# Shared gating steps moved into the routing chain of a macaron MoE kernel, with the rank product and the Exp moved to fit

## The chip, the cores and the metric

One core of a Trainium2 chip runs the whole program. The metric is the device time of one execution in microseconds (us); lower is better. The engines are TensorE (PE in the profile, PEld for its weight loads), VectorE (DVE), ScalarE (ACT), GpSimd (POOL) and the DMA queues, which SyncE (SP) and GpSimd fill. Each engine runs its own instructions in their written order and waits on semaphores that others raise.

## The reference

The input is 16 sequences of 256 tokens with 128 features, 4096 tokens in all. Three residual blocks follow each other:

```
x = x + 0.5 * ffn(layernorm(x))
x = x + attn(layernorm(x))
x = x + 0.5 * ffn(layernorm(x))

def ffn(h):                               # the same weights both times
    probs = softmax(h @ gate_W.T)         # 8 experts
    top_v, top_i = top_k(probs, 2)
    routed = sum over the 2 chosen experts e of
             top_v * (silu(h @ w1_e) * (h @ w3_e)) @ w2_e      # 128 -> 512 -> 128
    shared = (silu(h @ w1_s) * (h @ w3_s)) @ w2_s / 8          # 8 shared experts, 512 wide together
    return 0.5 * shared + 0.5 * routed
```

The attention is a linear one with running sums; the change does not touch it.

## The kernel before

The 4096 tokens lie in 32 tiles of 128, and 4 tiles are a chunk, so there are 8 chunks. The two feed-forward layers (l = 0 and 1 in the code, the first and the second layer here) have the same stages:

1. **Normalise and score.** Each chunk is normalised (DVE), transposed (PE), copied (ACT), multiplied with the gate (PE), and its scores are copied to `logit` (ACT). ACT and POOL split the transposed tokens into a high and a low part (`high_xnT`, `low_xnT`).
2. **The front.** Two kinds of work are interleaved. One is the shared expert in steps: a step k is one chunk times one quarter of the 512 hidden features. PE makes six matmuls for it (`in_shared`: three into psG, three into psU), ACT takes Silu of psG (`silu_shared`), DVE multiplies Silu by psU (`gated_shared`, reached by `shared_steps`), and after four steps PE makes the out-product of the chunk (`out_shared`, 32 matmuls), which DVE adds to X (`add_shared`). PE starts step k only when the Silu and the product of step k-2 are done, since psG and psU have two buffers. The other is routing: DVE finds the largest and second largest score of each token (`first_of` and its neighbours), PE counts ranks (`rank`), DVE turns ranks into slots (`slots_of`), 16 batches of one-hot matrices (DVE `batch`, ACT `pairs`, PE `batch`) put each token's number into its slot, and `table` and `experts` make the lists from them. In the first layer DVE also makes eight low parts of the routed weights behind the table (`low_part`), one per step, out of eight high parts that ACT made (W13H, L1213).
3. **The routed stage.** POOL fetches token rows by the table, PE transposes and multiplies them with the weights that ACT copies out of W13H and W13L (`weights_of`, L1229), and POOL sends the results back.
4. The last steps of the shared expert (4 in the first layer, 8 in the second) cover the tail.

The front has 28 steps in the first layer, of which 4 are done during the normalisation (`TAKEN` = 4 and 0), and 24 in the second. The order is written out by hand with constants. `PLAN` gives after which step DVE makes which batches (16 in 11 steps); ACT makes its part one step later, and PE takes the batches up `PLAN_LAG` = 3 steps later. `TABLE_STEP` is the step after which DVE makes the table. `RANK_STEP` is the step of PE at which `rank` stands; `out_shared` of the chunk c stands on PE at step 4c + 5. `Chain.then` lets DVE wait for each routing operation before the next.

Within the DVE chain of routing the kernel before has 2 shared steps between the maxima, 1 behind the gates (the softmax sum, its reciprocal and two products, L819 to L822) and 1 in `slots_of`. On ACT the two Exp of the scores stand behind the first Silu of the front (L1200 to L1203), in front of the second. On PE:

```
if 5 <= k < front[l] + 5:
    out_shared(Step.of(k - 5, 2 * FT))
if k == RANK_STEP[l]:        # 5 and 3
    rank()
```

Of the kernel before, what the change touches and what calls it, by code (L numbers as in the profile page):

```python
# [14 lines left out]
D = 128  # L15
# [39 lines left out]
RANK_STEP = [5, 3]  # L55

PLAN = [{n + 4 + step: 2 - step % 2 if step < 10 else 1 for step in range(11)} for n in TAKEN]
PLAN_LAG = 3
TABLE_STEP = [n + 15 for n in TAKEN]
# [36 lines left out]
ALU = mybir.AluOpType  # L96
# [66 lines left out]
def macaron(nc, x, w_qkvT, w_swigluT, w_outT, gateT, w1_e, w3_e, w2_e, w1_s, w3_s, w2_s, out):  # L163
    ctx = ExitStack()
    with ctx:
# [542 lines left out]
        def _(dve):  # L708
# [34 lines left out]
            for l in range(2):  # L743
# [47 lines left out]
                def first_of(k, scores):  # L791
# [11 lines left out]
                dve.wait_ge(shifted, l + 1)  # L803
                first_of(0, cand[:, :, :])
# [7 lines left out]
                first_of(1, logit[:, :, :])  # L812
                route.then(dve.tensor_tensor(chosen[:, :, :].rearrange("p e i -> p i e"), onehot[0][:, :, :],
# [4 lines left out]
                dve.wait_ge(expd, l + 1)  # L818
                route.then(dve.tensor_reduce(row_a[:, :], prob[:, :, :], X_AXIS, ALU.add))  # L819
                route.then(dve.reciprocal(row_b[:, :], row_a[:, :]))  # L820
                dve.tensor_scalar(XN[:, :, D], row_b[:, :], 0.25, None, ALU.mult)
                dve.scalar_tensor_tensor(XN[:, :, D + 1], row_b[:, :], 0.25, second_exp[:, :], ALU.mult, ALU.mult)\  # L822
                   .then_inc(gates_done, 1)
                shared_steps(1)

                def slots_of():
# [19 lines left out]
                    for k in range(TOPK):  # L846
                        route.then(dve.tensor_tensor(pick[:, :, :], cum[:, :, :].rearrange("p e i -> p i e"),
                                                     onehot[k][:, :, :], ALU.mult))
                        route.then(dve.tensor_reduce(posf[:, k, :], pick[:, :, :], X_AXIS, ALU.add))
                    route.then(dve.tensor_copy(pos[:, :, :], posf[:, :, :]))  # L850
# [83 lines left out]
                for k in range(SHARED):  # L934
                    if k == front[l] + 6 % FT:
                        copy_xT(Step.of(0, 2 * GT))
                    if k == done[0]:
                        shared_steps(1)
                    for _ in range(PLAN[l].get(k, 0)):
                        batch(taken)  # L940
                        taken += 1
                    if k == TABLE_STEP[l]:
                        table()
                        experts()
                    if l == 0 and 0 < k - TABLE_STEP[0] <= 2 * WPARTS:
                        low_part(k - TABLE_STEP[0] - 1)

# [180 lines left out]
        def _(act):  # L1128
            act.wait_ge(consts, CONSTS)
            for l in range(2):  # L1130
# [56 lines left out]
                else:  # L1187
                    high = 0
                    for c in range(TURNED, CHUNKS + 1):
# [6 lines left out]
                        high += 1  # L1196
                    silu_shared(taken)
                    for c in range(high, CHUNKS):
                        high_xnT(Step.of(c, 2))
                act.wait_ge(second_found, l + 1)  # L1200
                act.wait_ge(shifted, l + 1)
                act.activation(prob[:, :, :], cand[:, :, :], ACT.Exp)
                act.activation(second_exp[:, :], second[:, :], ACT.Exp).then_inc(expd, 1)  # L1203
# [3 lines left out]
                for k in range(taken + 1, SHARED):  # L1207
# [3 lines left out]
                    if l == 0 and part < 2 * WPARTS:  # L1211
                        cols = bass.ds(part // 2 * WCOLS, WCOLS)
                        act.activation(W13H[:, part % 2, cols], W13[:, part % 2, cols], ACT.Copy).then_inc(high_made, 1)  # L1213
                    for _ in range(PLAN[l].get(k - 1, 0)):
                        pairs(batches)
                        batches += 1
# [111 lines left out]
        def _(pe):  # L1328
# [19 lines left out]
            for l in range(2):  # L1348
# [88 lines left out]
                for k in range(taken, SHARED + 1):  # L1437
# [3 lines left out]
                    if k < front[l]:  # L1441
                        in_shared(Step.of(k, 2 * FT))
                    if k == front[l] + 1:
# [3 lines left out]
                    if k == RANK_STEP[l]:  # L1447
                        rank()
# [215 lines left out]
```

## Time and profile before

| | us |
|---|---|
| median of 3 runs | 735.5 |
| lowest and highest run | 734.17 and 737.56 |
| span of the profiled execution, first to last instruction | 733.5 |

The profile gives for its own execution the span only; the median of the runs lies 2.0 us above it, and the profile does not tell how much of that lies around the span. Over the span PE is busy 660.3 us (90%), DVE 458.8 (63%), ACT 411.3 (56%) and POOL 430.6 (59%). The first layer's front lies at about 36 to 112 us, its routed stage follows to about 301 us, attention to about 431 us, the second layer's front at 440 to 512 us, and its routed stage to about 701 us.

Times are read on the axis of the span. A timeline row gives the start, the length, the engine, the line and, in brackets, how long the engine stood idle before it and what released it. The length reaches to the end of the last result; on DVE and ACT the next instruction can start somewhat before that.

### The profile page before, as it was taken

What the parts mean: (1) busy time and instruction counts of PE and PEld (TensorE: products, weight loads), DVE (VectorE), ACT (ScalarE), POOL (GpSimd) and SP (SyncE); (2) the same over time, 40 slices, a digit from 0 to 9 for tenths busy, and PEclk for the clock granted to TensorE, in tenths of its full rate; (3) what the DMA queues carried; (4) which work ended last, traced back from release to release, by engine and by line L of the source; (5) the groups of instructions that cost most, each with busy time, mean ns of one, the idle gap of its engine ahead of it and who ended that gap; (6) DMA issues with size and microseconds to landing.
All of it is one profiled execution on the core that took longest, in us unless ns stands there. A gap on an engine that the chain in (4) does not pass through costs nothing.

```text
span 733.5 us, 14294 instructions
## 1 busy us (share of the span) xinstructions
PE 660.3 (90%) x4860; PEld 602.1 (82%) x4860; DVE 458.8 (63%) x1177; ACT 411.3 (56%) x861; POOL 430.6 (59%) x511
## 2 busy tenths in 40 slices
PE   3878999999999999957987777999999999999995
PEld 3767879999999999825654574888999999999983
DVE  6678895554445555359999867884555555544536
ACT  2658617666666666236654436664666666666520
POOL 5600075777777776489987424007577777777530
PEclk9989999999999999989999997999999999999999
DMA  9542011221222231131100002402212212212137
GB/s 296 231 78 40 1 42 38 56 52 52 52 55 52 52 53 44 57 105 44 47 12 1 0 1 46 73 2 49 40 55 54 52 52 56 51 53 52 43 104 261
DMA packets 35685, 45.91 MB, mean 63 GB/s; under 512 B 6432, under 2 KB 27936, under 8 KB 35232
## 3 DMA queue, kind: packets, MB, share of 16 engines
q1 hardware_dynamic: 25632, 24.39, 11.8%
q0 software_dynamic: 9984, 20.63, 11.5%
q8 instruction: 40, 0.66, 0.4%
q14 instruction: 29, 0.24, 0.1%
HBM read 28.41 MB, written 16.58 MB: 61 GB/s over the span
## 4 chain that ended last, share of the span: by engine, by line
PE 65%; DVE 20%; issue 4%; ACT 4%; POOL 3%; DMA 2%; SPq 1%; ACTq 0%; POOLq 0%; DVEq 0%
PE psY L1487 18%; PE psG L1334 6%; PE psU L1336 6%; PE psG L1336 6%; PE psU L1335 6%; PE psG L1335 6%; PE psU L1334 6%; PE psH L1405 4%; DVE rec L1076 3%; PE psT L1433 2%; DVE hs L748 2%; DVE XN L738 2%; DVE ln_stats L725 1%; DVE xn L1060 1%; POOL results L641 1%
## 5 line engine op out<-in xcount | busy, mean ns | idle before, releaser
L626 POOL DMA_INDIRECT rows<-tokens,source x156 | 153.7, 985 | 156.3 <-DVE source L900 98.6
L1155 ACT ACTIVATE silu<-psG 128x512 f32<-128x512 f32 x220 | 131.1, 596 | 150.6 <-PE psG L1336 147.2
L954 DVE TENSOR_TENSOR hT<-silu,psU 128x512 f32<-128x512 f32 x156 | 107.4, 688 | 158.9 <-PE psU L1336 150.3
L641 POOL DMA_INDIRECT results<-yout,target x156 | 153.8, 986 | 63.3 <-issue 45.7
L1487 PE MATMUL psY<-W,hT 128*128 x1232 | 162.4, 275 | 1.8 <-DVE yout L980 1.8
L1487 PEld LDWEIGHTS psY<-W,hT 128*128 128x128 f32 x1232 | 150.4, 191 | 2.2 <-DVE hT L954 2.2
L1229 ACT ACTIVATE w_high<-W13H 128x1024 fp32r x78 | 82.7, 1061 | 59.0 <-PE psU L1336 54.8
L1334 PE MATMUL psG<-xTH,w_high 128*128 128x256 f32 x312 | 100.0, 321 | 0.7 <-ACT w_low L1229 0.7
L1336 PE MATMUL psG<-xTH,w_low 128*128 128x256 f32 x312 | 88.0, 282 | 0.0
L1336 PE MATMUL psU<-xTH,w_low 128*128 128x256 f32 x312 | 88.0, 282 | 0.0
L1335 PE MATMUL psU<-xTL,w_high 128*128 128x256 f32 x312 | 87.7, 281 | 0.0
L1335 PE MATMUL psG<-xTL,w_high 128*128 128x256 f32 x312 | 87.4, 280 | 0.0
L1334 PE MATMUL psU<-xTH,w_high 128*128 128x256 f32 x312 | 86.9, 278 | 0.0
L1229 ACT ACTIVATE w_low<-W13L 128x1024 fp32r x78 | 81.8, 1048 | 0.0
L748 DVE TENSOR_TENSOR hs<-silu,psU 128x512 f32<-128x512 f32 x64 | 43.7, 684 | 38.3 <-PE psU L1336 30.5
L1405 PEld LDWEIGHTS psH<-W2S,hs 128*128 128x128 f32 x512 | 59.4, 192 | 5.7 <-DVE hs L748 4.7
L1405 PE MATMUL psH<-W2S,hs 128*128 128x128 f32 x512 | 60.1, 276 | 2.9 <-DVE hs L748 2.9
L1334 PEld LDWEIGHTS psG<-xTH,w_high 128*128 128x128 f32 x312 | 59.2, 190 | 0.9 <-issue 0.9
L1335 PEld LDWEIGHTS psG<-xTL,w_high 128*128 128x128 f32 x312 | 59.3, 190 | 0.0
L1334 PEld LDWEIGHTS psU<-xTH,w_high 128*128 128x128 f32 x312 | 59.1, 190 | 0.0
L1336 PEld LDWEIGHTS psG<-xTH,w_low 128*128 128x128 f32 x312 | 58.8, 188 | 0.0
L1335 PEld LDWEIGHTS psU<-xTL,w_high 128*128 128x128 f32 x312 | 58.6, 188 | 0.0
(188 smaller groups left out, 1215.7 us busy)
## 6 DMA issues: line engine op xcount, KB each, us to landing
W<-w_e SPq DMA_DIRECT2D x3, 2048.0 KB, 13.7
tokens<-XN SPq DMA_DIRECT2D x16, 260.0 KB, 5.9
Y<-results SPq DMA_DIRECT2D x32, 128.0 KB, 2.2
YF<-results SPq DMA_DIRECT2D x16, 256.0 KB, 5.9
rows<-tokens,source POOLq DMA_INDIRECT x156
results<-yout,target POOLq DMA_INDIRECT x156, 2.3
X<-x SPq DMA_DIRECT2D x8, 256.0 KB, 5.5
out<-X SPq DMA_DIRECT2D x8, 256.0 KB, 2.8
```

The source lines that it names most:

```text
L626: pool.indirect_dma_start(rows[:, slot(l, g), t, :], None, tokens, bass.IndirectOffsetOnAxis(ap=source[:, tile:tile + 1], axis=0))\
L641: pool.indirect_dma_start(results, bass.IndirectOffsetOnAxis(ap=target[:, tile:tile + 1], axis=0), yout[:, g % 2, t, :], None).then_inc(y_ ...
L748: dve.tensor_tensor(hidden, silu[:, s.u % 2, :], psU[:, s.u % 2, :], ALU.mult).then_inc(h_done, 1)
L954: dve.tensor_tensor(hT[:, s.u // PT % 2, half, :].rearrange("p f c -> p (f c)"), silu[:, s.u % 2, :], psU[:, s.u % 2, :], ALU.mult).then_i ...
L1076: dve.reciprocal(rec[:, s.u, :, :], den[:, s.u, :, :]).then_inc(y_link, 1)
L1155: act.activation(silu[:, s.u % 2, :], psG[:, s.u % 2, :], ACT.Silu).then_inc(silu_done, 1)
L1229: act.activation(used[p % 2][:, :, :], kept[:, :, bass.ds(entries[p], F)], ACT.Copy)\
L1334: pe.matmul(out, a_high, b_high, start=True, stop=False)
L1335: pe.matmul(out, a_high, b_low, start=False, stop=False)
L1336: return pe.matmul(out, a_low, b_high, start=False, stop=True)
L1405: i = pe.matmul(psH[:, par, t * D:(t + 1) * D], hs[:, par, f, t * P:(t + 1) * P], W2S[:, f, :], start=(f == 0), stop=(f == FT - 1))
L1487: i = pe.matmul(into[:, t * D:(t + 1) * D], hT[:, s.u // PT % 2, f, s.u % PT * P:(s.u % PT + 1) * P], W2[:, bass.ds(at + f * D, D)], start ...
```

## The change

`WOVEN` = 7 shared steps stand in the routing chain of DVE instead of 4: one more ahead of the first `first_of`, one more behind the second, and one more between the two choices in `slots_of`; the step that stood behind the gates now stands behind `picked`. The batches, the table and all that follows come 3 steps later (`PLAN`, `TABLE_STEP`). `rank` moves on PE to the steps 9 and 5 and stands ahead of that step's out-product. In the first layer the Exp move on ACT behind the Silu of step 10, and the gates on DVE behind the batch of step 12. In the second layer one more `high_xnT` and then the one Exp of `cand` stand ahead of the first Silu; the second choice's exponential is no longer an Exp but is picked out of `prob` by two DVE operations, in front of the gates.

```diff
-RANK_STEP = [5, 3]
-
-PLAN = [{n + 4 + step: 2 - step % 2 if step < 10 else 1 for step in range(11)} for n in TAKEN]
+WOVEN = 7
+RANK_STEP = [n + 5 for n in TAKEN]
+
+EXP_STEP = TAKEN[0] + WOVEN - 1
+GATES_STEP = EXP_STEP + 2
+
+PLAN = [{n + WOVEN + step: 2 - step % 2 if step < 10 else 1 for step in range(11)} for n in TAKEN]
 PLAN_LAG = 3
-TABLE_STEP = [n + 15 for n in TAKEN]
+TABLE_STEP = [n + WOVEN + 11 for n in TAKEN]
...
                 dve.wait_ge(shifted, l + 1)
+                shared_steps(1)
                 first_of(0, cand[:, :, :])
...
                 first_of(1, logit[:, :, :])
+                shared_steps(1)
...
-                dve.wait_ge(expd, l + 1)
-                route.then(dve.tensor_reduce(row_a[:, :], prob[:, :, :], X_AXIS, ALU.add))
...
+                def gates():
+
+                    dve.wait_ge(expd, l + 1)
+                    if l == 1:
+                        route.then(dve.tensor_tensor(pick[:, :, :], onehot[1][:, :, :], prob[:, :, :], ALU.mult))
+                        route.then(dve.tensor_reduce(second_exp[:, :], pick[:, :, :], X_AXIS, ALU.add))
+                    route.then(dve.tensor_reduce(row_a[:, :], prob[:, :, :], X_AXIS, ALU.add))
...
                 shared_steps(1)
+                if l == 1:
+                    gates()
...
+                        if k == 0:
+                            shared_steps(1)
...
+                    if l == 0 and k == GATES_STEP:
+                        gates()
...
+                    high_xnT(Step.of(high, 2))
+                    high += 1
+
+                    act.wait_ge(shifted, l + 1)
+                    act.activation(prob[:, :, :], cand[:, :, :], ACT.Exp).then_inc(expd, 1)
                     silu_shared(taken)
...
-                act.wait_ge(second_found, l + 1)
-                act.wait_ge(shifted, l + 1)
-                act.activation(prob[:, :, :], cand[:, :, :], ACT.Exp)
-                act.activation(second_exp[:, :], second[:, :], ACT.Exp).then_inc(expd, 1)
...
+                    if l == 0 and k == EXP_STEP:
+                        exponents()
...
+                    if k == RANK_STEP[l]:
+                        rank()
                     if k == front[l] + 1:
                         transpose_rows(Step.of(0, 2 * GT))
                     if 5 <= k < front[l] + 5:
                         out_shared(Step.of(k - 5, 2 * FT))
-                    if k == RANK_STEP[l]:
-                        rank()
```

## Rows read from the trace of the kernel before

**Rows 1.** Page part 4: shares of the chain of work that ended last, by engine.
```profile
PE 65%; DVE 20%; issue 4%; ACT 4%; POOL 3%; DMA 2%; SPq 1%; ACTq 0%; POOLq 0%; DVEq 0%
```

**Rows 2.** Stretches: start:end length, busy PE PEld DVE ACT POOL, clock, DMA share, GB/s.
```profile
41.70:46.40 4.70, 0.01 (x1) 0.00 (x0) 3.10 (x8) 2.28 (x3) 0.00 (x0) 0.89 0.00 0
46.40:52.00 5.60, 5.58 (x15) 4.43 (x16) 3.23 (x13) 2.83 (x4) 0.00 (x0) 0.50 0.72 153
449.40:458.20 8.80, 8.32 (x20) 5.38 (x21) 8.19 (x24) 2.22 (x4) 0.84 (x1) 0.50 0.44 92
```

**Rows 3.** Timeline, first layer (start, length, engine, line, what, count, [idle before <-releaser]).
```profile
40.60 0.42 ACT L1202 ACTIVATE prob<-cand 128x256 f32<-128x256 f32 x1 [1.55 <-DVE second L808]
43.13 0.69 DVE L748 TENSOR_TENSOR hs<-silu,psU 128x512 f32<-128x512 f32 x1 [2.11 <-ACT silu L1155]
46.41 0.19 PE L1412 MATMUL psY<-chosen_rows,before 128*128 128x8 bf16 x1 [4.71 <-DVE chosen_rows L816]
62.54 0.43 PE L1421 MATMUL psT<-pair,at_place 128*128 128x156 bf16 x4 [0.64 <-ACT pair L1168]
```

**Rows 4.** Timeline, second layer, VectorE, ScalarE and TensorE at the start of the front.
```profile
441.51 1.41 DVE L793 SCALAR_TENSOR_TENSOR pick<-cand,rev_e 128x256 f32<-128x256 f32 x1
447.45 1.28 ACT L1155 ACT_TABLE_LOAD   x1
449.39 0.79 PE L1334 MATMUL psG<-XNTH,W13SH 128*128 128x512 f32 x1 [3.83 <-ACT silu L1155]
460.65 0.48 DVE L866 TENSOR_TENSOR in_tile<-column,pos_part 128x312 bf16<-128x312 bf16 x1
463.47 0.72 PE L1421 MATMUL psT<-pair,at_place 128*128 128x156 bf16 x8
```

**Rows 5.** Timeline, first layer, from the last batch to the first routed matmul.
```profile
88.18 0.45 PE L1421 MATMUL psT<-pair,at_place 128*128 128x156 bf16 x4
88.67 0.24 DVE L889 COPY is_choice<-psT 128x78 f32<-128x78 f32 x1 [1.01 <-PE psT L1421]
92.19 0.69 DVE L748 TENSOR_TENSOR hs<-silu,psU 128x512 f32<-128x512 f32 x1
92.80 1.22 DVE L908 TENSOR_TENSOR W13L<-W,W13H 128x1024 fp32r<-128x1024 f32 x1
107.75 1.22 DVE L908 TENSOR_TENSOR W13L<-W,W13H 128x1024 fp32r<-128x1024 f32 x1
110.17 1.06 ACT L1229 ACTIVATE w_high<-W13H 128x1024 fp32r x1 [4.14 <-issue]
112.42 0.36 PE L1334 MATMUL psG<-xTH,w_high 128*128 128x256 f32 x1 [0.70 <-ACT w_low L1229]
```

**Rows 6.** Timeline, TensorE: an out-product, two steps, and the same end in layer 2.
```profile
89.90 3.73 PE L1405 MATMUL psH<-W2S,hs 128*128 128x128 f32 x32
93.39 0.48 PE L1334 MATMUL psG<-XNTH,W13SH 128*128 128x512 f32 x1
94.86 0.39 PE L1334 MATMUL psG<-XNTH,W13SH 128*128 128x512 f32 x1
490.57 0.45 PE L1421 MATMUL psT<-pair,at_place 128*128 128x156 bf16 x4
512.30 0.36 PE L1334 MATMUL psG<-xTH,w_high 128*128 128x256 f32 x1
```

**Rows 7.** Groups by line: busy us, mean ns | idle before, releasers.
```profile
L1155 ACT ACTIVATE silu<-psG 128x512 f32<-128x512 f32 x220 | 131.1, 596 | 150.6 <-PE psG L1336 147.2 <-DVE hs L748 3.2
L1213 ACT ACTIVATE W13H<-W 128x1024 fp32r<-128x1024 f32 x8 | 8.4, 1050 | 0.0
L1273 ACT ACT_TABLE_LOAD x1 | 1.3, 1283 | 0.0
```

**Rows 8.** Attention: timeline row of a wait, and the stretch right behind it.
```profile
385.82 0.44 PE L1539 MATMUL psT<-ident,xn 128*128 128x128 f32 x2 [2.36 <-DVE xn L1060]
385.82:387.00 1.18, 0.70 (x3) 0.47 (x4) 1.15 (x8) 0.38 (x1) 1.18 (x2) 0.86 0.07 14
```

More of the change, by code:

```diff
@@ L816, in _ @@
                 dve.tensor_copy(chosen_rows[:, :], base[:, :]).then_inc(picked, 1)
-                dve.wait_ge(expd, l + 1)
-                route.then(dve.tensor_reduce(row_a[:, :], prob[:, :, :], X_AXIS, ALU.add))
[L820 to L823, printed above, removed]
+                def gates():
[4 more added lines that the diff above has]
+                    route.then(dve.tensor_reduce(row_a[:, :], prob[:, :, :], X_AXIS, ALU.add))
+                    route.then(dve.reciprocal(row_b[:, :], row_a[:, :]))
+                    dve.tensor_scalar(XN[:, :, D], row_b[:, :], 0.25, None, ALU.mult)
+                    dve.scalar_tensor_tensor(XN[:, :, D + 1], row_b[:, :], 0.25, second_exp[:, :], ALU.mult, ALU.mult)\
+                       .then_inc(gates_done, 1)
                 shared_steps(1)
+                if l == 1:
+                    gates()
                 def slots_of():
@@ L1199, in _, with exponents @@
                         high_xnT(Step.of(c, 2))
-                act.wait_ge(second_found, l + 1)
-                act.wait_ge(shifted, l + 1)
-                act.activation(prob[:, :, :], cand[:, :, :], ACT.Exp)
-                act.activation(second_exp[:, :], second[:, :], ACT.Exp).then_inc(expd, 1)
+                def exponents():
+                    act.wait_ge(shifted, l + 1)
+                    act.wait_ge(second_found, l + 1)
+                    act.activation(prob[:, :, :], cand[:, :, :], ACT.Exp)
+                    act.activation(second_exp[:, :], second[:, :], ACT.Exp).then_inc(expd, 1)
                 if l == 0:
```

## The prediction

> **What bounds the kernel now.** I read the page first: the chain that ended last is 65% TensorE and 20% VectorE [rows 1]. Then I read the busy time by stretch, to find where TensorE stands. In the first layer it stands for the whole of 41.70 to 46.40, and behind that it runs 5.60 us at a granted clock of 0.50, its lower level (1.2 of 2.4 GHz) [rows 2]. That costs about half of 5.60, so 2.8 us. The timeline says why: `rank` waited 4.71 us for the DVE chain, and that chain had itself stood 2.11 us for a Silu that was queued behind the Exp of the scores and the table load [rows 3]. In the second layer TensorE stands 3.83 us for the second Silu, which again is queued behind two Exp and their loads [rows 4], and 8.80 us follow at clock 0.50 [rows 2]. So the change aims at real waits. But a wait of TensorE counts only if what ends the front is TensorE. In the first layer it is not quite: the first routed matmul at 112.42 waits for ACT's weight copy, which waited for the last low part of DVE [rows 5]. In the second layer it is TensorE's own queue, 512.30 [rows 6].
>
> **Prices of the parts.** On TensorE a step is 94.86 - 93.39 = 1.47 us (1.37 behind another step) and an out-product 93.39 - 89.90 = 3.49 [rows 6]. On DVE a shared step takes 92.80 - 92.19 = 0.6 until the next instruction [rows 5]; `add_shared` has the same shape and I give it 0.6 too. On ACT a Silu is 0.60, a W13H part 1.05 [rows 7], a table load 1.28 [rows 4], the Exp 0.42 [rows 3]. Nothing else is computed anew but two DVE operations in the second layer.
>
> **First layer, up to the last batch.** Now DVE makes step 4 ahead of the first maximum and step 5 behind it, so TensorE can go on with steps 6 to 9 during the chain. `rank` moves behind step 9; I get the ranks' input ready about 0.5 us after TensorE arrives, instead of 4.71. That gives 4.2, and the slow stretch of 2.8 goes with it. The waits of 0.64 for a batch, one of which stands in [rows 3] (there are four), mostly go, since DVE now has more lead: 2. Against this stands a new wait: ACT has Silu 10, W13H part, load, two Exp, load in front of Silu 11. Step 10 can start only behind the out-product of chunk 1, at about 51; Silu 10 starts at 52.0, and adding 0.5 + 0.95 + 1.28 + 0.6 + 1.28 + 0.6 gives 57.2. TensorE has finished step 12 at 55.3 and stands 1.9. The gates on DVE cost nothing there (1.1 us, DVE then waits for TensorE anyway); if that cover is gone, they cost 1.1. Sum: 4.2 + 2.8 + 2 - 1.9 = 7.1, bounds 5 and 9. Three steps and one out-product more stand ahead of the last batch than before: 3 x 1.4 + 3.5 = 7.7. So the last batch comes at about 88.2 + 0.6 = 88.8 by these terms; walking all four queues forward row by row I get 88.1. I take 88.2, the same moment as before [rows 5], but with 7.7 us less of TensorE work left behind it.
>
> **First layer, behind the last batch.** This is where the gain is lost. DVE starts the table 0.5 us behind the batch and needs 92.19 - 88.67 = 3.5 us for table and experts [rows 5]. Before, TensorE had an out-product right behind one step to cover that. Now step 24 and the psG half of step 25 follow (2.3 us), and its psU half wants the product of step 23, which DVE makes behind the table, done 4.8 us behind the batch. TensorE stands about 2.4. Then the eight low parts: they follow the table, one per step, and the table is not earlier. From 92.1 on DVE has 5 products (3.0), 8 low parts of 1.14 (9.1), two `add_shared` (1.2), `copy_xT` (1.4, which now stands ahead of the last low part) and a wait of 1.3 for step 26: 16.0, so it ends at 108.1. Before it was 107.75 + 1.14 = 108.9. From there to the routed stage it was 112.42 - 108.9 = 3.5 (the register load, two weight copies) [rows 5], so the routed stage starts at 111.7, 0.7 earlier. TensorE has finished at about 105.3 and stands 6.4 us. After its waits of 4.71 and 3.83 the clock was at its lower level for 5.60 and 8.80 [rows 2, 3, 4]; behind 6.4 us it will be again, now in the routed stage, where TensorE works without a gap. I take 5.3 us at half speed, 2.6 lost; bounds 1.7 and 4.4 (half of 8.80). First layer: -0.7 + 2.6 = +1.9, from +0.5 to +4.
>
> **Second layer.** ACT starts Exp as soon as `cand` is there (441.5), still with the table that attention's Exp and Tanh used: its group of lines shows one load in all for both [rows 7]. Then one load instead of three. Silu 0 is done at 443.7 and not at 443.0, and DVE now waits for it ahead of the first maximum: 2.2. The chain from 441.51 to the first batch at 460.65 is 19.1 [rows 4]. Out of it goes the wait for the Silu of 2.8; into it come that 2.2, three steps 1.8, an `add_shared` 0.6, and the two operations of the second exponential 1.1 (by the routing operations of that shape, 0.6 and 0.45; 0.9 to 2.1, as the pick took 1.41 where it ran beside GpSimd [rows 4]). That makes 22.0 and the first batch at 463.5. TensorE takes step 9 behind the product of step 7, out-product 1 behind that, and batches from 467.9 on, 10 steps and 2 out-products done, against 463.47 with 7 steps and 1 out-product [rows 4]. From there to the last batch it took 27.1 [rows 4, 6]; with its small waits mostly gone I take 26, so 493.9. Then step 20, half of step 21, a wait of 2.3 as in the first layer, the other half, an out-product, steps 22 and 23, the transposes, a wait of 0.5, an out-product: 1.5 + 0.7 + 2.3 + 0.7 + 3.5 + 2.8 + 0.4 + 0.5 + 3.5 + 0.2 = 16.1, so 510.0 against 512.30. Walked by the same prices, the kernel before gives 511.2 and not 512.30, as the walk leaves part of the slow clock out. I take -2.0, bounds -2.8 and -1.
>
> The Trainium skill (ScalarE: Activation LUTs, What ACT_TABLE_LOAD costs) gives a switch of tables 1283 ns and a drain of 1380 ns, 2.66 us in all. The trace shows the load with 1.28 and the next function right behind it, no drain. By the page, each of the two loads removed in the second layer would free ACT 1.4 us more, and the wait of 1.9 at Silu 11 would be longer; by the row neither holds, and no term above uses it.
>
> **Sum.** +1.9 - 2.0 = -0.1. What lies behind each front (routed stage, attention, tail) is the same work in the same order and moves as a whole. The profiled execution has a span of 733.5, the median is 735.5 and the 2.0 between them I carry over: 735.4 for the median.
>
> **Rivals.**
> - *The clock also falls at the table.* Each of the two waits of 2.3 to 2.4 us could do what 2.36 did in attention, where after a short operation and another small wait the clock was 0.86 over the next 1.18 us and so on its way down [rows 8]. For it speaks that row; against it, that here dense work stands on both sides. It costs 2.6 to 3.6 per layer: 738 to 739 for one, 742 for both. Chance 0.19, of which 0.05 for both.
> - *The chain of low parts is not the bound, or is quicker.* If ACT and DVE were ready when TensorE is (105.3), the first layer would give -7.1 with no slow clock: 726. Against it stand eight low parts behind a table that is not earlier, and [rows 5], where they already were the last to come. Chance 0.05.
> - *The wait ahead of the routed stage stays without a slow clock.* Then -0.7 - 2.0: 732.8. All waits over 3 us in the rows speak against. Chance 0.09.
> - *The change doesn't shorten the first wait*, because the chain gets each added step at its full 0.6 and more, and ranks come late: the last batch 2 to 3 us later, 738. Chance 0.05.
>
> **How the numbers follow.** The forecast itself has 0.62: 733.5 to 737.5, by the bounds of the two layers. The range for 8 in 10 takes in the one slow clock at the table and the case without any: 732.2 to 739.8. A measurement of this kernel can tell about 0.5%, 3.7 us. Faster by more than that: the second rival and a corner of the third, with the forecast's lower end, 0.10. Slower by more: both slow clocks, half of the one, and a part of the last rival, 0.17. Within: 0.73.
>
> **What would show it.** In the changed profile: TensorE's wait for `chosen_rows` under 1 us in both layers and clock 1.00 at 46 to 52 and 449 to 458; a wait for Silu 11 of about 2; two waits for the product behind the table of about 2.3; the last low part ending near 108; TensorE standing about 6 us ahead of the first routed matmul at 111 to 112.5, and a clock of 0.50 behind it; the second layer's front some 2 us shorter. It would be wrong if the last batch of the first layer came more than 2 us from 88.2, or if the low parts were not what the routed stage waits for.

## The result, and the profile after

| | before | after |
|---|---|---|
| median, us | 734.84 (4 runs, 734.17 to 737.56) | 740.95 (4 runs, 740.03 to 743.15) |
| ratio | | 1.0088, 95% interval 1.0069 to 1.0106 |
| profiled execution: time and span | span 733.5 | 743.15, span 741.4 |
| first routed matmul, first layer | 112.42 | 116.30 |
| end of the first routed stage (last `yout` wait of PE) | 300.07 | 305.37 |
| XN of the second layer to its first routed matmul | 77.98 | 78.88 |

The change made the kernel 6.1 us slower. The forecast was no change. In the profiled executions 5.3 of the 7.9 us between the spans arise in the first layer and 0.9 in the second (78.88 - 77.98); another 1.65 lie in the tail, where this one execution, the slowest of the four, had a stretch of clock 0.50 at 724 that the other did not have.

What the change was to remove, it removed. This is the timeline of the changed kernel, the rows that answer to [rows 3] and [rows 4]: PE's `rank` in both layers, and the first matmul behind Silu 11.

```profile
47.74 0.18 PE L1440 MATMUL psY<-chosen_rows,before 128*128 128x8 bf16 x1 [0.26 <-DVE chosen_rows L822]
...
57.72 0.50 PE L1362 MATMUL psG<-XNTH,W13SH 128*128 128x512 f32 x1 [1.96 <-ACT silu L1173]
...
459.42 0.18 PE L1440 MATMUL psY<-chosen_rows,before 128*128 128x8 bf16 x1 [0.24 <-DVE chosen_rows L822]
```

PE waits 0.26 us for the ranks' input where it waited 4.71, and 0.24 in the second layer. The new wait of 1.96 us for Silu 11 is the one that was forecast with 1.9. On ACT the reason for it can be read, one instruction behind the other:

```profile
53.93 1.28 ACT L1227 ACT_TABLE_LOAD   x1
55.22 0.42 ACT L1227 ACTIVATE prob<-cand 128x256 f32<-128x256 f32 x1
55.55 0.21 ACT L1228 ACTIVATE second_exp<-second 128x32 f32<-128x32 f32 x1
55.78 1.28 ACT L1173 ACT_TABLE_LOAD   x1
57.07 0.60 ACT L1173 ACTIVATE silu<-psG 128x512 f32<-128x512 f32 x1
```

What the forecast did not have is what came behind such waits. Here are the stretches of PE in the changed kernel. The columns are the stretch, its length, PE's busy time with the count of matmuls, the mean granted clock, and the DMA share with GB/s.

```profile
46.40:52.00 5.60, 5.33 (x41) 1.00 0.01 3
57.72:62.00 4.28, 4.28 (x17) 0.60 0.00 0
95.62:99.60 3.98, 3.98 (x17) 0.57 0.13 33
112.84:116.30 3.46, 0.00 (x1) 0.54 0.17 42
116.30:120.00 3.70, 3.70 (x17) 0.51 0.25 58
449.40:458.20 8.80, 5.71 (x21) 1.00 0.00 0
505.14:509.20 4.06, 4.05 (x18) 0.58 0.23 49
```

The stretches 46.40 to 52.00 and 449.40 to 458.20 had clock 0.50 before [rows 2] and have 1.00 now: that part is as forecast. But now the clock is at its lower level (1.2 of 2.4 GHz) behind the wait for Silu 11 (57.72), behind the table in both layers (95.62, 505.14) and at the start of the routed stage (116.30). Of these four only the last stood in the forecast. The waits behind the table, and the last low part with what follows it, are these rows (DVE, ACT and PE; they answer to [rows 5]):

```profile
91.39 0.24 DVE L905 COPY is_choice<-psT 128x78 f32<-128x78 f32 x1 [0.65 <-PE psT L1449]
...
95.62 0.51 PE L1362 MATMUL psU<-XNTH,W13SH 128*128 128x512 f32 x1 [2.15 <-DVE hs L752]
...
111.63 1.21 DVE L924 TENSOR_TENSOR W13L<-W,W13H 128x1024 fp32r<-128x1024 f32 x1
...
114.05 1.06 ACT L1257 ACTIVATE w_high<-W13H 128x1024 fp32r x1 [9.52 <-issue]
...
116.30 0.55 PE L1362 MATMUL psG<-xTH,w_high 128*128 128x256 f32 x1 [6.10 <-ACT w_low L1257]
...
505.14 0.50 PE L1362 MATMUL psU<-XNTH,W13SH 128*128 128x512 f32 x1 [2.15 <-DVE hs L752]
```

The table starts at 91.39, 2.7 us later than before, and the last low part ends at 112.84 instead of 108.97. PE stands 6.10 us for it.

### The profile page after: what moved, and what is told of

It reads as the page before. It is cut to its first block, busy times and chain, and to the rows that moved or that the text cites. A ratio compares the mean times of both kernels' runs of the same rounds, so it can differ in the third digit from the quotient of the medians.

```text
span 741.4 us, 14290 instructions
## 1 busy us (share of the span) xinstructions
PE 664.4 (90%) x4860; PEld 604.6 (82%) x4860; DVE 459.0 (62%) x1179; ACT 407.0 (55%) x858; POOL 431.0 (58%) x511
## 4 chain that ended last, share of the span: by engine, by line
PE 67%; DVE 19%; issue 3%; POOL 3%; ACT 3%; DMA 3%; SPq 1%; ACTq 0%; POOLq 0%; DVEq 0%
PE psY L1515 18%; PE psH L1433 6%; PE psG L1362 6%; PE psU L1364 6%; PE psU L1363 6%; PE psG L1364 6%; PE psU L1362 6%; PE psG L1363 6%; DVE rec L1094 3%; PE psT L1461 2%; DVE XN L742 2%; DVE hs L752 2%; DVE ln_stats L729 1%; DVE xn L1078 1%; PE psT L1449 1%
## 5 line engine op out<-in xcount | busy, mean ns | idle before, releaser
L1364 PE MATMUL psU<-xTH,w_low 128*128 128x256 f32 x312 | 88.2, 283 | 0.0
L1433 PEld LDWEIGHTS psH<-W2S,hs 128*128 128x128 f32 x512 | 63.3, 202 | 5.4 <-DVE hs L752 3.5
L1433 PE MATMUL psH<-W2S,hs 128*128 128x128 f32 x512 | 63.8, 286 | 2.6 <-DVE hs L752 2.6
```

The source lines that it names most:

```text
L1364: return pe.matmul(out, a_low, b_high, start=False, stop=True)
L1433: i = pe.matmul(psH[:, par, t * D:(t + 1) * D], hs[:, par, f, t * P:(t + 1) * P], W2S[:, f, :], start=(f == 0), stop=(f == FT - 1))
```

## The experiments

My theory after the result: the waits are those of the forecast, and the time went into the clock behind the short ones; the eight low parts then carry each delay on to the start of the routed stage. Rivals: the second layer, or DVE's work itself, is what got longer. All ratios below are against runs of the kernel before on the same chip, whose medians were 734.95 to 735.12. A ratio is estimated from all runs of the two kernels and is not exactly the quotient of their medians. Times "against the changed kernel" compare medians across chips with its 740.95, which itself rests on four runs that spread by 3 us.

**One layer at a time.** The constants and orders of the change became a choice by layer (NEW); the edit is shown in part:

```
-WOVEN = 7
+NEW = (True, False)              # (False, True) for the second layer only
+WOVEN = [7 if new else 4 for new in NEW]
-RANK_STEP = [n + 5 for n in TAKEN]
+RANK_STEP = [n + 5 if new else o for n, o, new in zip(TAKEN, (5, 3), NEW)]
...
```

> The change in the first layer only; the second layer is as before. Theory (the sizes were off, the mechanism was right: waits of about 2 us that TensorE meets behind Silu 10 and behind the table let its clock fall): first routed matmul near 116.3 (112.42 before), routed stage ends 5.3 us later than before, median about 740. Rival A (most of the loss is the second layer's, since its wait behind the table costs more than its front gains): median within 1.5 us of before. Rival B (noise of the clock in attention and in the tail): both single-layer kernels within 2 us of before.

Measured 739.48 us, ratio 1.0056 (1.0039 to 1.0073). Its waits and their places are those of the changed kernel:

```profile
58.08 0.50 PE L1370 MATMUL psG<-XNTH,W13SH 128*128 128x512 f32 x1 [1.96 <-ACT silu L1178]
...
95.92 0.53 PE L1370 MATMUL psU<-XNTH,W13SH 128*128 128x512 f32 x1 [2.15 <-DVE hs L753]
...
116.59 0.55 PE L1370 MATMUL psG<-xTH,w_high 128*128 128x256 f32 x1 [6.10 <-ACT w_low L1265]
```

> The change in the second layer only; the first layer is as before. Theory: +1.0 us, median about 736, since the front is 1.3 us shorter up to its last batch's lead but the clock falls behind the table's wait. Rival A: +4 us or more, median 739 or above. Rival B (clock at the table has no part in it): -2 us, as forecast, with the wait of 2.15 us there but clock 1.00 behind it.

Measured 735.88 us, ratio 1.0011 (0.9993 to 1.0029). In this kernel the first layer's table load waited for `second` and no longer for `cand`, so `rank` came at 47.94 instead of 46.41 and the first layer was about 1.5 us longer. The number alone did not settle the second layer; the next run had the two waits in their old order.

> The change in the second layer only, with the two waits of the first layer's table load in the order of the kernel before, so that the first layer's trace should be that of the kernel before (rank at 46.41 behind a wait of 4.71, first routed matmul at 112.42). Theory (the second layer's change costs what its table wait and slow clock cost: from XN of 434.32 to the end of its routed stage 265.40 us in the kernel before, 266.30 in the changed kernel): 735.5 to 736.5 us, ratio 1.001 to 1.002. Rival (as I forecast, the second layer is 1 to 2.8 us shorter, and the changed kernel's profile only had a bad clock there): 732.5 to 734 us.

Measured 735.74 us, ratio 1.0001 (0.9989 to 1.0013), `rank` at 45.95. By the interval the second layer's change gives or takes less than 1 us. So it does not give the 2 us forecast, and it does not explain the loss. Most of the loss belongs to the first layer: 739.48 - 735.07 = 4.4 of the 6.1 us, by the run with the first layer only. The two layers alone add up to 5.1 us; the last 1.0 is within the spread of the changed kernel's four runs.

**The Exp one step earlier.**

```
-EXP_STEP = TAKEN[0] + WOVEN - 1
-GATES_STEP = EXP_STEP + 2
+EXP_STEP = TAKEN[0] + WOVEN - 2
+GATES_STEP = EXP_STEP + 3
```

> The changed kernel, but the first layer's Exp stand on ScalarE behind Silu 9 and its W13H part, one step earlier, where ScalarE stood 4.10 us; the gates stay at step 12. Theory: TensorE's wait of 1.96 us for Silu 11 goes and with it the stretch at clock 0.50 at 58.6 to 62.0 (1.7 us lost); the last batch of the first layer comes at about 87.5 instead of 90.91, and the routed stage 3.4 us earlier, median about 737.5. Rival (the wait for Silu 11 is covered by VectorE, whose batches set the pace behind it): last batch at 90 to 91, median 740 to 741.

Measured 736.45 us, ratio 1.0018 (0.9997 to 1.0039): 4.5 us less than the changed kernel. The wait for Silu 11 and its stretch of clock 0.50 are gone, the table starts at 88.71, the waits of 2.16 and 6.10 stay. So the two Exp, moved by one step, take back most of the loss. In the profile the first routed matmul comes at 113.55, 2.75 us earlier than in the changed kernel and not the 3.4 expected, and about 1.4 us of the difference lie in the tail, which this move does not touch; the 4.5 us between the medians are more than the move itself shows.

**The low parts on GpSimd.** `low_part` is taken out of DVE's queue and made by GpSimd, with the same operands:

```
+                if l == 0:
+                    for j in range(2 * WPARTS):
+                        w, cols = j % 2, bass.ds(j // 2 * WCOLS, WCOLS)
+                        pool.wait_ge(high_made, j + 1)
+                        pool.tensor_tensor(W13L[:, w, cols], W13[:, w, cols], W13H[:, w, cols].bitcast(fp32),
+                                           ALU.subtract).then_inc(w_split, 1)
...
```

> The changed kernel, but the eight low parts of the routed weights are made by GpSimd, which is idle there, as soon as ScalarE has made the high parts; VectorE makes none. Theory (the chain of low parts behind the table, then the weight copies, sets the start of the routed stage): TensorE's wait of 6.10 us ahead of the first routed matmul goes, and the clock stays at 1.00; first routed matmul at about 110 instead of 116.3, median about 733.5. Rival (that wait only hides another: the fetch of rows or the weight copies themselves, or GpSimd's long subtractions slow VectorE by as much): first routed matmul at 114 or later, median 739 or above.

Measured 739.78 us, ratio 1.0089 (1.0054 to 1.0124). The wait of 6.10 is gone, and nothing is won: DVE's operations take longer beside GpSimd's subtractions, the table starts at 101.64 instead of 91.39 and the first routed matmul comes at 117.63. Two queues of this run:

```profile
66.06 5.00 POOL L625 TENSOR_TENSOR W13L<-W,W13H 128x1024 fp32r<-128x1024 f32 x2 [2.32 <-ACT W13H L1236]
...
66.44 5.01 DVE L891 TENSOR_SCALAR at_place<-column,pos_part 128x128 bf16<-128x128 bf16 x4
...
71.75 0.73 DVE L891 TENSOR_SCALAR at_place<-column,pos_part 128x128 bf16<-128x128 bf16 x4
```

The same four operations of a batch take 5.01 us beside GpSimd and 0.73 alone. The rival of this run held, so it says nothing on the low parts. The Trainium skill (GPSIMD Engine Reference, Specifications) says that GpSimd shares its SBUF interfaces with VectorE and that they contend when VectorE runs in a 2-port mode or has two SBUF inputs. The rows agree that VectorE is held up beside GpSimd (5.01 against 0.73); in which mode it ran they do not show.

**The low parts spread out.** They stay on DVE but no longer stand one per step behind the table:

```
+LOW_STEP = {13: 1, 17: 1, 21: 2, 23: 1, 24: 1, 25: 1, 26: 1}
...
-                    if l == 0 and 0 < k - TABLE_STEP[0] <= 2 * WPARTS:
-                        low_part(k - TABLE_STEP[0] - 1)
+                    for _ in range(LOW_STEP.get(k, 0) if l == 0 else 0):
+                        low_part(lows)
+                        lows += 1
```

> The changed kernel with the eight low parts of the routed weights (DVE, 1.22 us each) no longer one per step behind the table, but at steps 13, 17, 21 (two) ahead of it and 23 to 26 behind it. The same instructions. Theory (ahead of the routed stage TensorE waits 6.10 us for the last low part, at 111.63, and the slow clock of 6.8 us behind it follows from that wait): the last low part ends about 4 us earlier, the wait falls to 2 us or less, and the stretch of clock 0.50 at 113.2 gets shorter or goes; the first routed matmul comes at 111 to 113 instead of 116.30, and up to 1.5 us of slow clock are saved behind it; the second layer is unchanged: 735 to 738 us. Rival (DVE has no slack ahead of the table either: each low part there pushes the batches back by its 1.2 us): last batch 3 to 5 us later than 90.91, waits of TensorE for the batches, maybe with a slow clock, first routed matmul at 114 to 117: 739 to 742 us.

Measured 733.0 us, ratio 0.9965 (0.9948 to 0.9983), below the range I gave. The last low part starts at 104.16 instead of 111.63, the routed stage at 109.62 instead of 116.30, and PE does not wait there:

```profile
104.16 1.21 DVE L925 TENSOR_TENSOR W13L<-W,W13H 128x1024 fp32r<-128x1024 f32 x1
...
109.62 0.36 PE L1364 MATMUL psG<-xTH,w_high 128*128 128x256 f32 x1
```

The rival (no slack on DVE ahead of the table) fell: the table starts at 91.06, against 91.39. The control is the same move in the kernel before:

```
+LOW_STEP = {10: 1, 14: 1, 18: 2, 20: 1, 21: 1, 22: 1, 23: 1}
```

> The kernel before, with nothing of the change, and its eight low parts at steps 10, 14, 18 (two), 20 to 23 instead of 20 to 27: the same offsets to its TABLE_STEP of 19 as in the run with the spread low parts. Theory (what low parts spread out can give is TensorE's wait ahead of the routed stage, which is 0.70 us in the kernel before and 6.10 in the changed one): 734 to 736 us, so that the 8 us that this move gave the changed kernel belong to the two together. Rival (the low parts hold something up in the kernel before too, and most of the gain is theirs alone): 728 to 732 us.

Measured 733.74 us, ratio 0.9978 (0.9967 to 0.9988), just below the 734 to 736 expected. So the same move gives the kernel before 1.3 us and the changed kernel 8: in the first one PE stands 0.70 us ahead of the routed stage ([rows 5]), in the second one 6.10. These low parts hid part of the gain of the change, but they were not all that stood in its way: with them spread out in both kernels the change is worth 0.7 us (733.00 against 733.74), and the intervals of the two ratios overlap. The changed kernel with its low parts spread out still has its slow clock behind the waits for Silu 11 (58.0), behind the table (95.6) and in the second layer (498.3).

**The out-product behind the table.** On PE the out-product that stood in front of the last batch moves behind the step that waits for the table. Its `add_shared` moves with it on DVE, which is not shown:

```
-                    if 5 <= k < front[l] + 5:
+                    if OUT_MOVED[l] and k == TABLE_STEP[l] + 2:
+                        out_shared(Step.of(TABLE_STEP[l] - 6, 2 * FT))
+                    if 5 <= k < front[l] + 5 and not (OUT_MOVED[l] and k == TABLE_STEP[l] - 1):
```

> The changed kernel with one out-product of the shared experts moved on TensorE, in each layer, from behind step TABLE_STEP - 1 to behind step TABLE_STEP + 2, and its add_shared moved with it on DVE. The same work in another order. TensorE then has 3.5 us of work while DVE makes the table, and its last batches come earlier. Theory (TensorE's queue sets the last batch, and the wait at the table costs itself and its slow clock): last batch of the first layer 1.5 to 3.5 us ahead of 90.91, wait of 2.15 gone in both layers and its two slow stretches with it, the low parts end 1.5 to 3.5 earlier; first layer -2 to -3.5, second -2 to -3.7: 734 to 737 us. Rival (DVE's chain of batches is nearly as late as TensorE, so that TensorE only waits for DVE at the batches instead): last batch less than 1 us earlier, waits of 1 to 3 us for the batches in place of that at the table, possibly with their own slow stretch: 739 to 741 us.

Measured 732.86 us, ratio 0.9969 (0.9950 to 0.9988), the table at 86.63, no wait of 2.15 in either layer. The theory's direction held and its size was too small: 734 to 737 us were expected, and the last batch came at 86.14, 4.8 us earlier, where 1.5 to 3.5 were expected. Part of that may be luck of this execution, whose wait of 1.95 for Silu 11 had no slow clock behind it (the last section shows the rows).

**Filling waits.** These runs leave the waits as they are and put matmuls into them whose results are not used. The first fills the two waits at the table:

```
+                    if s.first == TABLE_STEP[l] + 3:
+                        pe.wait_ge(ranks_read, l + 1)
+                        for _ in range(FILL[l]):          # 9
+                            pe.matmul(psY[:, :], W13SH[:, 0, tile], XNTH[:, chunk], start=True, stop=True)
```

> The changed kernel with nine more TensorE matmuls (128x128 by 128x512, the size of one part of a step's product) at step TABLE_STEP + 3, between the step's psG and its psU, in both layers. Their results are not used; nothing else is changed. In the changed kernel TensorE stands 2.15 us at that place, and the granted clock is 0.50 for 3.4 us from 0.1 to 0.5 us behind the end of that wait (96.1 and 505.7). Nine matmuls take about 2.1 us, so the product behind the table is ready when they end. Theory (the clock falls because TensorE stood 2.15 us): no wait over 0.5 us there, no stretch of clock 0.50 at 96 and at 506. What it is worth: up to 1.7 us in each layer on TensorE (half of 3.4), less where DVE's low parts set the start of the routed stage, so 0 to 1.7 in the first and 1 to 1.7 in the second layer: 737.5 to 740 us. Rival (the clock falls there for another cause, such as the load of the last 100 us): the slow stretches stay within 1 us of their places and the time is 741 to 742.

Measured 737.87 us, ratio 1.0035 (1.0020 to 1.0049): more work and 3.1 us less time than the changed kernel. Its clock behind the two filled waits:

```profile
95.00:99.00 4.00, 3.91 (x32) 1.00 0.15 33
504.70:509.00 4.30, 4.21 (x34) 1.00 0.23 50
```

The changed kernel had 0.57 and 0.58 there. The rival (another cause for the clock) fell. The next one adds eight matmuls at step 13 and 25 ahead of the routed stage (7 in the runs `filled_four_waits_b` and `filled_four_waits_c`):

```
+                    if l == 0 and s.first == 13:
+                        for _ in range(8):
+                            pe.matmul(psY[:, :], W13SH[:, 0, tile], XNTH[:, chunk], start=True, stop=True)
...
+                if l == 0:
+                    for _ in range(25):
+                        pe.matmul(psY[:, :], W2S[:, 0, :], W2S[:, :, :].rearrange("p f d -> p (f d)"), start=True, stop=True)
                 pe.wait_ge(w_off_done, l + 1)
```

> The run with the filled table waits, and fills at two more places of the first layer: eight matmuls ahead of step 13 (where TensorE stood 1.95 us for Silu 11, with a clock of 0.50 for 3.4 us from 57.6) and 25 ahead of the routed stage (where it stood 6.10 us, with a clock of 0.50 for 6.8 us from 112.2). 0.24 us each, so 1.9 and 6.0 us of matmuls whose results are not used. No wait is shortened: each one is only filled. Theory (each wait costs itself and a slow clock behind it, and only the second part goes here): no stretch of clock 0.50 from 50 to 300; 1.5 us less at step 13, of which a part is kept at the routed stage, and 1.4 us less behind the start of the routed stage (its time from first matmul to last was 189.07 us in the changed kernel with the slow clock and 187.65 in the kernel before without), so 2 to 3 us less than 737.87: 735 to 736 us, about the time of the kernel before. Rival (the fills are not long enough or late, or the clock falls for another cause): a slow stretch stays at 58 or at 112, and the time is 737 to 739.

Measured 751.76 us, ratio 1.0232 (1.0217 to 1.0247). I sized the last fill by the wrong row: with these operands one took 0.86 us (50 passes in 21.62 us), and the routed stage started at 129.32. The profile still tells one thing: without a stretch of clock 0.50 that stage took 317.06 - 129.32 = 187.74 us, against 305.37 - 116.30 = 189.07 in the changed kernel.

> As the run with four filled waits, but with 7 in place of 25 matmuls ahead of the routed stage: there 50 passes took 21.62 us, since those operands run at 0.86 us for one and not at 0.24, so the first routed matmul came at 129.32. 7 of them take 6.0 us. Theory (every wait keeps its length, every slow clock behind the four waits goes): no clock of 0.50 from 50 to 300, first routed matmul between 113 and 115, last of the first routed stage 187.7 us behind it, median 735 to 736.5, so that nearly all of the 5.5 to 6 us between the changed kernel and the kernel before is slow clock. Rival (the first routed matmul comes later than 115 because the fill delays it, or the clock falls after all): 737 to 739.

Measured 739.54 us, ratio 1.0062 (1.0041 to 1.0084), outside the 735 to 736.5 expected, though the clock and the first routed matmul (114.59) came as expected. The eight matmuls of step 13 stood behind the wait for Silu 11 and not ahead of it, so they filled nothing and added 2.1 us of work. The same is true of this run:

> The changed kernel with only the fill of eight matmuls ahead of step 13 of the first layer (TensorE stands 1.96 us there and a clock of 0.50 for 3.4 us follows at 58.6). Theory (half of 3.4 us is lost there, and it is kept by everything behind it, up to the last low part and the routed stage): no slow stretch at 58, last batch 1 to 1.5 us ahead of 90.91, median 739 to 740. Rival (what is saved at 58 is lost again at the low parts or at the table, whose own slow stretches stay): last batch 1 us earlier or less, median 740.5 to 741.5.

Measured 742.34 us, ratio 1.0078 (1.0047 to 1.0109). That is above both expected ranges, and its question stays unanswered. With the eight ahead of the wait:

> As filled_four_waits_b, with the eight matmuls of step 13 now in front of the wait for Silu 11. In the two runs before they stood behind it, so that they lengthened the wait of 1.95 us by 2.1 us of work. Theory (all that the fills remove is slow clock): no wait over 0.5 us at step 13, no clock of 0.50 from 50 to 300, last batch at 89 to 90, first routed matmul at 112 to 113.5, the end of the first routed stage 187.7 behind it, median 735 to 737. That would be 4 to 6 of the 5.9 us between the changed kernel and the kernel before. Rival (the clock is a small part, and TensorE's queue or DVE's chain ends late by itself): first routed matmul at 114 or later, median 738 to 740.

Measured 736.85 us, ratio 1.0022 (1.0007 to 1.0036). Its profile has no clock of 0.50 between 50 and 300 us:

```profile
57.40:62.00 4.60, 4.50 (x33) 1.00 0.00 0
93.00:99.00 6.00, 5.91 (x43) 1.00 0.14 33
112.88:120.00 7.12, 7.12 (x59) 1.00 0.19 47
```

The other rows that count are the start of its table, its last low part and the first routed matmul:

```profile
89.59 0.24 DVE L905 COPY is_choice<-psT 128x78 f32<-128x78 f32 x1 [0.65 <-PE psT L1458]
...
108.21 1.21 DVE L924 TENSOR_TENSOR W13L<-W,W13H 128x1024 fp32r<-128x1024 f32 x1
...
112.88 0.36 PE L1362 MATMUL psG<-xTH,w_high 128*128 128x256 f32 x1
```

The first layer ends at 300.52, 0.45 us behind the kernel before and 4.85 ahead of the changed kernel. So of the 5.3 us that the first layer lost, 4.85 are slow clock and what follows from it. In the medians the fills give 4.1 of the 6.1 us. The ratio of 1.0022 leaves about 1.7 us. In its profile 0.7 us more than in the kernel before lie between the first routed stage and the second layer, where PE's first wait in attention is 5.41 and not 4.93. The stretch of clock 0.50 behind it is longer too, 10.2 us against 6.8, but the changed kernel has that as well and loses only 0.05 there. Another 1.4 lie in the second routed stage, where PE has a wait of 1.14 for `yout` that only `filled_four_waits_b` has as well (1.11). The cause of neither is shown.

> The changed kernel with only the fill of seven matmuls ahead of the first layer's routed stage, which cover its wait of 6.10 us; their results are not used. Theory (the slow clock of 6.8 us behind this wait costs what the stage's own length says, 189.07 against 187.65 us): no clock of 0.50 from 110 to 300, 1.4 us less than the changed kernel, 739 to 740. Rival (as forecast from half of 5.3 us, 2.6 less): 738 to 739. If the fill delays the stage instead, 741 or more.

Measured 737.78 us, ratio 1.0044 (1.0024 to 1.0064), 3.2 us less than the changed kernel, more than either theory said. Its profile shows why I can't take this as the share of the routed wait: the wait for Silu 11 is the same 1.96 us, but no slow clock follows it, and the table wait of the second layer is the same 2.16 and again none follows.

```profile
57.35:62.00 4.65, 4.65 (x34) 1.00 0.00 0
93.67:97.20 3.53, 3.53 (x14) 0.52 0.16 38
...
500.54:504.50 3.96, 3.96 (x32) 1.00 0.23 55
```

The routed stage's own length is the better measure: 187.6 us here, so 1.4 for the slow clock at its start.

**All three moves together.** Exp one step earlier, low parts spread out, out-product behind the table, with the edits above.

> The changed kernel with three moves together: Exp of the first layer one step earlier (this gave 4.5 us by itself, since the 1.96 us wait for Silu 11 and its slow stretch went), one out-product of each layer behind the table, and the low parts spread out. The same computation. Theory (each of the waits costs itself and its slow clock, and what bounds the start of the routed stage is the last low part): no TensorE wait over 1.5 us between 50 us and the first routed matmul, no clock of 0.50 from 58 to 112, first routed matmul at 105 to 109 instead of 116.30, second layer 2 to 3.5 us shorter: 727 to 732 us, which would be ahead of the kernel before at 735. Rival (DVE has no slack ahead of the table, so the low parts there and the earlier place of the batches on TensorE only turn the waits into others): 733 to 737 us.

Measured 724.05 us, ratio 0.9849 (0.9823 to 0.9875), 1.5% faster than the kernel before and below my range. The last low part starts at 99.24, the first routed matmul at 104.70 (before: 112.42 in [rows 5]), and neither front has a stretch of clock 0.50 left:

```profile
99.24 1.21 DVE L930 TENSOR_TENSOR W13L<-W,W13H 128x1024 fp32r<-128x1024 f32 x1
...
104.70 0.36 PE L1369 MATMUL psG<-xTH,w_high 128*128 128x256 f32 x1
```

> The run with all three moves, but the second layer as in the kernel before. It tells how much of the 11 us between 724.05 and the kernel before belongs to the first layer. Theory (the first routed matmul at 104.70 against 112.42 gives 7.7, and the second layer the rest): 727 to 728 us. Rival (the second layer's change gives nothing even with its table wait covered, and the rest is the clock): 724 to 725 us.

Measured 727.18 us, ratio 0.9894 (0.9879 to 0.9908). The first layer gives 7.9 us, and the second 3.1 once its table wait is covered. So the order that the change brings can be worth more than the one before it, with these three moves beside it. How much of the 11 us is the change and how much the moves is not shown: of the three, only the low parts were tried in the kernel before (1.3 us), and the out-product behind the table was not.

## Why the prediction was wrong

The step that failed is the price of the short waits: the sum took the waits of 1.9 for Silu 11 and of 2.3 to 2.4 behind the table as idle time only, with no slow clock behind them. The runs showed a clock of 0.50 for 3.4 us behind each, and with the waits filled 4.85 of the 5.3 us that the first layer lost came back.

- *First layer up to the last batch.* Forecast: table at 88.7. Measured: 91.39, 2.7 us late. The wait terms are right (0.26 for `rank`, 1.96 against 1.9 for Silu 11, no clock of 0.50 at 46 to 52). The step that failed is the term "stands 1.9" for that wait: it had no clock behind it. The run with the four filled waits puts the table at 89.59, and the one with the routed wait filled, which had no slow clock there, at 89.44; so the slow clock makes 1.8 of the 2.7. Of the other 0.9, 0.6 is what I took off when I chose 88.2 for the last batch, from the walk, and not the 88.8 of the sum of the terms. That the batch came at 90.91, more than 2 us from 88.2, is the sign of being wrong that the prediction named.
- *Behind the last batch.* Forecast 23.0 us from the table to the first routed matmul; measured 24.91 in the changed kernel and 23.29 with the waits filled. Again 1.6 is clock, behind the wait of 2.15 (forecast 2.4), and the walk was off by 0.3. PE's wait of 6.10 was forecast with 6.4, and the low parts as the bound were right: the run with the low parts spread out shows it.
- *The slow clock in the routed stage* was forecast with 2.6, bounds 1.7 to 4.4. It cost 1.4, by 189.07 against 187.65 (and 187.74 filled). The clock had fallen by 113.1, while PE still stood, and rose at 119.9, so only 3.6 us of it lay under work and not 5.3.
- *First layer in sum.* Forecast +1.9, bounds +0.5 to +4; measured +5.3 = 1.9 + 2.7 + 1.9 - 1.2, by the three points above. The error is in the bounds: they had no case with two short waits that each lower the clock.
- *Second layer.* Forecast -2.0, bounds -2.8 and -1; measured +0.9 in the profile, and a ratio of 1.0001 in the run of the second layer alone. Its rows: DVE waits 2.45 for Silu 0 (forecast 2.2), the pick takes 1.48, the table starts 1.2 us late at 500.91 (forecast 493.9 + 0.5, plus the 5.35 by which the layer starts later), and behind it the clock of 0.50 at 505.7. In the run with the routed wait filled, where that stretch and the one at the layer's start did not occur, the same instructions take 512.28 - 436.40 = 75.88 us, 3.0 less for two stretches of 3.4. That is 2.1 less than the 77.98 of the kernel before, near the 2.0 forecast; but that kernel had a stretch at the layer's start too (434.5), so this is no clean confirmation.
- *Rivals.* "The clock also falls at the table", both layers, had 0.05 of chance and gave 742; that is near what came (740.95), with a third place that I had not listed at Silu 11. What led me wrong was the argument against it, that dense work stands on both sides of the wait. The runs do not bear it out. [Rows 8] were the evidence, a fall behind 2.36 us, and I let them count for too little. The three other rivals fell. The last of them had its sign, a last batch 2 to 3 us late, but not its cause: the ranks came at 47.74 with a wait of 0.26.

Where part of a gain rests on the clock (2.8 of the 7.1 in the first layer), every wait of the changed order has to be priced by the clock as well; I did so for one wait of four.

## What to carry to other kernels

When a change removes one long wait of TensorE and leaves two short ones, price each new wait twice: as idle time, and as about 1.5 us of slow clock behind it, and fill or cover the waits (an independent product moved behind the one that waits) before judging the change. A gain on TensorE's queue can be held back by the other engines' fixed work ahead of the next stage, here eight subtractions of 1.2 us behind the table. It arrives when that work is moved early as well (worth 1.3 us without the change and 8 with it) or when what it stands behind comes earlier (the out-product behind the table, also 8). Fills whose results are not used tell idle time from clock, if they stand in front of the wait and are sized by a row with the same operands.

## What the runs showed of the hardware

Waits of about 2 us lower the clock, but not each time. The wait of 1.95 to 1.96 us for Silu stands in ten of the traces, in dense work. In five a clock of 0.50 for 3.4 us follows it, in five none, and the engine's work in front of it is the same in most of them. Behind the wait the changed kernel had 0.60 over 57.72 to 62.00 (above). This is the same stretch in the run with the out-product moved, whose queue differs only later:

```profile
57.62:62.00 4.38, 4.38 (x32) 1.00 0.00 0
```

It holds 32 matmuls, the other 17, and both are six of a step and then those of an out-product. Of fifteen waits of 2.15 to 2.16 at the table, eleven had a stretch of 3.4 us at or behind them. Of the eight that were filled (four runs, two layers) none had. Every wait of the fronts from 3.8 to 6.1 us had a stretch of 3.4 to 10.2 us at or around it. The Trainium skill (TensorE: Matmul & The Clock Gate, Part 1) says that one and the same kernel has a different number of slow matmuls at its start from run to run, by the gate's phase. The ten traces fit that, though they are of ten kernels, one each, and of a place in mid-kernel; no run here repeats one kernel's trace. By these counts one profile can neither price such a wait nor clear it.

The table load was 1.28 us, and the next function started directly behind it (53.93, 55.22; 55.78, 57.07). The Trainium skill (ScalarE: Activation LUTs, What ACT_TABLE_LOAD costs) adds a drain of 1380 ns to the load. These rows do not show it, and for this kernel they decide.
